# Interleaving the tree block of each token group with the state-space scans of the later groups

## The reference

```
a = in-projection of LN(x); convolution, silu; dt = softplus(...)
for every channel d (256) and state n (16), along the 256 tokens:
    h = exp(dt * A[d,n]) * h + dt * B[n] * u        # the scans
    y[d] += C[n] * h
out1 = LN(x + W_out (y + D*u) * silu(z))

gate = sigmoid(q @ routers.T)                        # the tree, 255 nodes
lp   = product of 8 levels of gate or 1 - gate       # 256 leaves a token
out2 = (lp @ leaf_values) @ Wout + b

4 layers: retention with 8 heads, then gelu(LN(.) @ W1) @ W2
8 experts of one hidden layer, the best by softmax for each token
```

## Time and profile before

| | us |
|---|---|
| median of 3 runs (781.0 to 782.15) | 782.1 |
| the profiled execution, its own time | 781.24 |
| its span, first to last instruction | 779.4 |
| prologue, to the first scan | 76 |
| scans, first start to last end | 190 |
| from there to `rx_stats` of group 3 | 118 |
| from there to the end | 396 |

### The profile page before, as it was taken

How to read it: one execution, slowest core, us unless ns; L and a number is a source line. 1 busy time by engine, 2 the same in 40 slices (tenths; PEclk the granted TensorE clock), 3 DMA queues, 4 the chain that set the end, 5 groups by cost and what they waited for, 6 DMA issues and landing times. The chain is left out here.

```text
span 779.4 us, 13077 instructions
## 1 busy us (share of the span) xinstructions
PE 658.2 (84%) x4791; PEld 430.8 (55%) x4800; DVE 622.9 (80%) x1519; ACT 417.2 (54%) x729; POOL 429.1 (55%) x380
## 2 busy tenths in 40 slices
PE   4997798898988833748899999999999999899994
PEld 1444444444444332634667667777666666667773
DVE  6479798999989686467688888888888888779886
ACT  1996786776767305444454444444444444355551
POOL 6113587696887848464665555555555555551222
PEclk9997799999999986789999999999999999999997
DMA  9003132332344100000000000000000000000001
GB/s 324 7 5 54 35 100 89 86 96 81 84 100 85 55 2 0 0 1 1 2 1 22 1 6 15 22 2 4 15 2 21 2 7 13 1 1 1 1 25 32
DMA packets 17297, 27.36 MB, mean 35 GB/s; under 512 B 2320, under 2 KB 7056, under 8 KB 16976
## 3 DMA queue, kind: packets, MB, share of 16 engines
q1 hardware_dynamic: 17232, 26.51, 12.8%
HBM read 25.32 MB, written 1.18 MB: 34 GB/s over the span
## 5 line engine op out<-in xcount | busy, mean ns | idle before, releaser
L573 POOL TENSOR_TENSOR arena<-arena 128x1024 f32<-128x1024 f32 x64 | 150.0, 2359 | 52.3 <-PE psum L1322 27.3
L991 DVE TENSOR_TENSOR_SCAN arena<-arena,psum 128x1024 f32<-128x1024 f32 x64 | 141.8, 2267 | 3.3 <-issue 2.0
L1322 PE MATMUL psum<-arena,Cs 128*128 128x512 f32 x256 | 121.9, 599 | 1.2 <-POOL arena L573 1.2
L510 POOL TENSOR_TENSOR ve<-mv,eps 128x4 f32<-128x4 f32 x52 | 16.0, 307 | 191.7 <-DVE mv L889 191.7
L705 ACT ACTIVATE arena<-arena 128x510 f32<-128x510 f32 x128 | 84.8, 711 | 51.8 <-DVE arena L991 49.8
L620 POOL TENSOR_TENSOR arena<-arena,mhalf 128x32 f32<-128x32 f32 x16 | 86.8, 5428 | 2.3 <-DVE arena L1108 2.3
L1214 PE MATMUL psum<-Cs,arena 128*128 128x128 f32 x240 | 39.6, 290 | 42.9 <-ACT arena L748 25.9
L1407 PE MATMUL psum<-arena,Wl 128*128 128x512 f32 x128 | 67.4, 639 | 8.6 <-DVE arena L1092 5.3
L1322 PEld LDWEIGHTS psum<-arena,Cs 128*128 128x128 f32 x256 | 45.2, 191 | 46.3 <-issue 35.0
L1214 PEld LDWEIGHTS psum<-Cs,arena 128*128 128x128 f32 x240 | 28.6, 147 | 62.6 <-issue 28.3
L1305 PE MATMUL psum<-Cs,arena 128*128 128x128 f32 x256 | 35.2, 284 | 23.9 <-ACT arena L727 20.7
(11 more groups left out here) (172 smaller groups left out, 1415.6 us busy)
## 6 DMA issues: line engine op xcount, KB each, us to landing
arena<-c_rows_by_state SPq DMA_DIRECT2D x32, 512.0 KB, 4.8
Wl<-wl SPq DMA_DIRECT2D x4, 384.0 KB, 3.2
Wd<-wd SPq DMA_DIRECT2D x1, 1100.0 KB, 10.8
X<-x SPq DMA_DIRECT2D x4, 256.0 KB, 6.4
Sel<-sel SPq DMA_DIRECT2D x1, 1024.0 KB, 8.3
Wl<-wl SPq DMA_DIRECT2D x4, 256.0 KB, 3.0
out<-X SPq DMA_DIRECT2D x4, 256.0 KB, 2.3
Cs<-const SPq DMA_DIRECT2D x1, 614.0 KB, 9.2
```

The costliest lines, as they stand in the source:

```text
L573: pool.tensor_tensor(Hc[:, h], Hs[:, r, h], Crows[:, r], ALU.mult).then_inc(hc_ready, 1)
L991: dve.tensor_tensor_scan(Hs[:, turn % 2, h], Da[:, h], rows_of(turn, h), 0.0, ALU.mult, ALU.add).then_inc(scanned, 1)
L1322: ins = pe.matmul(bank[h], ident, Hc[:, h, group(e)], start=False, stop=False, skip_group_check=True)
```

## The change

**Order.** Scan steps enter `OPENING` as steps of their own, and tree steps are sorted among them: for groups 0 to 2 at 8(g+1) + 1.701 + 0.859 t turns, for group 3 at 33.29 + 0.586 t, where the scans end at 32. The first layer steps start at 31.087 + 3.988 (g + t). All engines follow this list. `TREE_SCHEDULE` has other offsets. `SCHEDULE` has small changes; the cyclic order of `LAYER` on each engine stays as it was.

**PSUM.** Two row buffers, banks 2+3 and 4+5. So the fill of step q+2 waits for scan q. Banks 6 and 7 are the tree's: 7 for `y_proj`, `b_turn`, `b_proj`, both for `logits` and `lp`. At step q PE now adds the states of q-1. `flip` moves from five fills ahead to directly before the last odd turn's fills, and the first one to the front. In the layers `rotate` uses banks 1, 4, 5, 7, and `mix` uses bank 6 alone.

**SBUF.** `Z`, `U`, `Dt`, `Dtu` are stored by group, and a finished group's pieces are used again: `Z` for `Bt` and `LpT`, `U` for `Gates`, `Dt` and `Dtu` for `LpA` and `LpB`; later ones for layer tensors. Shapes of instructions stay. POOL's clearing of `Va` (1.8 us) moves from the tree to before the first layer step.

```diff
+TREE_AT, TREE_PACE = 1.701, 0.859
+LAST_AT, LAST_PACE = 1.290, 0.586
+FIRST_STEPS_AT, FIRST_STEPS_SCALE = 31.087, 3.988
+OPENING = [(what, k, g, 0) for _, _, what, k, g in sorted(
+    [(turn + h / 2, 0, "scan", h, turn) for turn in range(ROUNDS + 1) for h in range(HALVES)]
+    + [(STATE_PAIRS * (g + 1) + TREE_AT + TREE_PACE * t, 1, what, 0, g) for g in range(G - 1) for t, what in TREE_SCHEDULE]
+    + [(STATE_PAIRS * G + LAST_AT + LAST_PACE * t, 1, what, 0, G - 1) for t, what in TREE_SCHEDULE]
+    + [(FIRST_STEPS_AT + FIRST_STEPS_SCALE * (g + t), 2, what, k, g) for g in range(G) for t, what, k in SCHEDULE if g + t < G])]
...
-        row_buffer = [psum[:, (2 + 2 * i) * GC:(4 + 2 * i) * GC] for i in range(3)]
+        row_buffer = [psum[:, (2 + 2 * i) * GC:(4 + 2 * i) * GC] for i in range(2)]
...
-            "rotate": ((1, rotated, 1), (4, rotated, 2), (5, rotated, 3), (1, rotated, 4)),
+            "rotate": ((1, rotated, 1), (4, rotated, 2), (5, rotated, 3), (7, rotated, 4)),
...
+            def scan_step(turn, h):       # PE
+                q = 2 * turn + h
+                if q + 2 < 2 * ROUNDS:
+                    n = FILL_OF[divmod(q + 2, 2)]
+                    if FILL_ORDER[n - 1][0] == "flip":
+                        fill(n - 1)
+                    fill(n)
+                if 1 <= q <= 2 * ROUNDS:
+                    of, half = divmod(q - 1, 2)
+                    if of % STATE_PAIRS == 0:
+                        skip_row(of // STATE_PAIRS, half)
+                    add_states(of, half)
...
                 if what == "b_proj":
                     pe.wait_ge(lp_rows, 2 * g + 2)
-                    if g >= 2:
-                        pe.wait_ge(t2_ready, g - 1)
-                    tokens(bank[6 + g % 2], [LpT[:, g, h, :] for h in range(2)], ...
+                    tokens(hold(7, t2_ready, g + 1), [LpT[g][:, h, :] for h in range(2)], ...
...
-                        pe.wait_ge(*yt_rows.at(layer, g - 2))
+                        rows_y = claim(what, 0, layer, g)
```

More of the change, by code:

```diff
@@ L219 @@
 TURNED = [t for t in range(ROUNDS) if t % 2 == 1]
-FLIP_AHEAD = 6
 def fill_order():
-    fills = []
-    for q in range(2 * ROUNDS):
-        turn, h = divmod(q, 2)
-        g, place = divmod(turn + FLIP_AHEAD // 2, STATE_PAIRS)
-        if h == 0 and place == 0 and 0 < g < G:
+    fills = [("flip", 0, 0)]
+    for turn in range(ROUNDS):
+        g = (turn + 1) // STATE_PAIRS
+        if (turn + 1) % STATE_PAIRS == 0 and g < G:
             fills.append(("flip", g, 0))
-        fills.append(("turned" if turn in TURNED else "rows", turn, h))
-        if q == 1:
-            fills.append(("flip", 0, 0))
+        fills += [("turned" if turn in TURNED else "rows", turn, h) for h in range(HALVES)]
     return fills
@@ L672, in _ @@
                     act.wait_ge(dtx_ready, 2 * g + h + 1)
-                    own.put(act.activation(Hs[:, 1, h, part], Dt[:, h, group(g)], ACT.Abs))
+                    own.put(act.activation(Hs[:, 1, h, part], Dt[g][:, h], ACT.Abs))
                 own.settle()
```

311 lines of the change are left out of this document (153 added, 158 removed).

## The result

| | before | after |
|---|---|---|
| median (us) | 781.97 (781.0 to 782.15, 4 runs) | 801.95 (800.65 to 805.62, 4 runs) |
| span of the profiled execution | 779.4 | 798.9 |
| end of the last scan | 265.7 | 335.5 |
| marker, `rx_stats` of group 3 | 383.2 | 406.9 |
| marker to the end of the span | 396.2 | 392.0 |

The ratio is 1.0255, 95% interval 1.0215 to 1.0295: the change makes the kernel 20 us slower. I had 774.5 and a range that ended at 789. The places were as foretold, their sizes were not. Against my sum the scans end 8.9 later (335.5 for 326.6), the way from there to the marker is 13.4 longer (71.4 for 58), and the layers gain 4.8 less (-4.2 for -9.0). That is 27.1 us, and 774.5 + 27.1 is 801.6.

A forecast was written before the change was run, and what follows sets the result against it. DVE was taken to bound the scans, PE the layers. Scan terms put the scans' end at 326.6; 58 more put the marker 1.4 later; layers -9.0 made -7.6: 773.6 profiled, 774.5 median, range 757 to 789.

The forecast's parts named there:

- Gates, -6.4: Scans: with PE adding one step behind, three gate waits of 2.1 go, -6.4 us (bounds -6.4 and 0).
- Two buffers +4, flips +4.5: Scans: two row buffers lose 0.4 us a pair in ten pairs, +4; three flips delay fills about 1.5 each, +4.5.
- `b_proj`, +8.8: Scans: DVE idles 4.4 us before `b_proj` of groups 0 and 1, waiting for PE, +8.8 (bounds 0 and 8.8).
- Tables, +4.2: Scans, at `logits`: ACT's sigmoid and exponential table loads make decays 2.1 us late, twice, +4.2 (bounds 0 and 7.4).
- Held-up instructions, +13.8: Scans: POOL's products hold up `g_norm` and `levels`, both inputs in SBUF, 2.75 us in each of five blocks, +13.8.
- slower rival: Scans: POOL lags behind queued powers and `low_levels`, two products hold each block, 11.8 more, 786.3 us; chance 0.22.
- Sum of the scans: Scans: 265.7 plus all scan terms, including +32 us of DVE's tree work, puts the last scan's end at 326.6.
- From the last scan to the marker, 58: Behind the scans: group 3's chain alone bounds the way, 58 us; 46 with nothing in the way, 70 with waits doubled.
- Layers, -9.0: Layers: the fourth `rotate` projection's bank wait goes, 0.69 us off each of 13 slots, -9.0 (bounds -9.0 and 0).
- Free gaps: Scans: POOL's products never lie beside `g_norm` and `levels`, so the 13.8 go, 760.7 us; chance 0.20.
- No gain in the layers: Layers: another wait takes the place of the bank's, so -9.0 falls away, 783.5 us, no change; chance 0.10.
- three signs that I had called wrong: Scans' end below 310 or above 340; scans waiting mostly for fills; a layer slot as long as before.

The follow-up runs named there:

- e9: The kernel before with e1's layer banks, and PE adding the states of step q-1 instead of q-2: 770.14 us, ratio 0.9860.
- e1: The kernel before with only the changed kernel's layer bank table (fourth `rotate` projection in bank 7, `mix` in bank 6): 777.00 us, ratio 0.9951.
- e14: The changed kernel with the flips in banks 6 and 7, taking no row buffer: 798.96 us, ratio 1.0226.
- e12: The kernel of e2 with the flips in banks 6 and 7, taking no row buffer: 783.73 us, ratio 1.0028.
- e2: The changed kernel with its whole tree behind the scans, in the order of the kernel before: 794.93 us, ratio 1.0194.
- e6: The changed kernel with the gates of groups 0 and 1 computed by exponential, so no table loads in the scans: 801.27 us, ratio 1.0274.
- e5: The changed kernel with `g_norm` of groups 0 to 2 reading `ln_g` and `ln_b` from PSUM bank 6 instead of SBUF: 794.15 us, ratio 1.0176.
- e10: The changed kernel with all first layer steps sorted behind the marker, `rx_stats` of group 3: 839.82 us, ratio 1.0759.
- e13: The kernel of e10 with matrix products of constants on PE where it stands idle: 832.36 us, ratio 1.0664.
- e3: The changed kernel with DVE's `b_proj` and `t2_stats` of groups 0 and 1 behind the next turn's first scan: 792.09 us, ratio 1.0163.
- e4: The changed kernel with 14 unused bf16 matmuls on PE ahead of each of five fills: 801.76 us, ratio 1.0278.

## Why the prediction was wrong

**What bounds the kernel.** Right. DVE sets the pace of the scans, so all of its tree work is added there: busy time grows by 50.1, of which 32 was foretold and is found. The scan stays at 2.26.

**Gates, -6.4.** Right: the lag of one step takes the 6.4 of waits away and shortens the scans by 7.0 with three buffers (e9 against e1). In the changed kernel the gates' waits fell to 0.8.

**Two buffers +4, flips +4.5.** Close in the changed kernel (9.5 more of waits for fills, flips 4.4 of it by e14), though by luck: without tree work beside them the two are 5.8 and 11.5 (e12, e2).

**`b_proj`, +8.8.** The step that failed is "PE's is behind a bf16 fill and an addition": there were two additions. It measured 11.9. Held to be the upper bound, it was not one.

**Tables, +4.2.** The wait is 4.3, as foretold. Taking it away is worth nothing (e6): other waits and held-up time fill it.

**Held-up instructions, +13.8.** The mechanism is shown (e5), the size was 17.6, and taking 13.2 of it away wins 7.7. Of the slower rival's 11.8 more, 3.8 came. In the rows at 235.60 and 239.87 DVE is held for 5.0: two of POOL's products and an addition of 128x512 (1.31) fall into the block. That happened in two blocks of five. POOL was late there because its product waited 2.21 for PE's addition (the row at 236.03), not because of powers queued among its products.

**Sum of the scans.** From 76.0 on, DVE was idle 11.8 us before (0.3 of the 12.1 lie behind the scans' end), so 26.9 were foretold, and 31.5 are found: +4.6. Busy 223.7 were foretold and 228.0 are found: +4.3, of which 3.8 is held-up time. Together +8.9.

**From the last scan to the marker, 58.** This is the step that failed worst, by 13.4: the chain of group 3 was sized too short. I put it at 46 with nothing in the way, and in the expectation of e10 at 50 with group 2's steps. Without any layer step in the way it took 64.9 (e10), and 60.4 with the granted clock mostly up (e13); in the changed kernel it is 71.4. The term "gates end at 5.8" measured 8.5, which is 2.7 of it. I took every PE step at its length at full clock, though the tree stretch before had a granted clock of 0.82; 1.7 us of that can be seen in the changed kernel. The last power, norm and addition, 5.0, measured 8.1 because layer steps fill DVE up to the marker. What remains is spread over the steps between, and its cause stays open. I named 70 as the bound "with each in-order wait doubled"; the true value was above even that.

**Layers, -9.0.** Half: 0.37 a slot instead of 0.69 (e1). The wait that I read, 0.93, is that of a weight load. PE itself was still at the third projection for a good part of it, so the step that failed is "so 0.69 comes off each slot".

**The rivals.** Free gaps: did not come. Slower: 3.8 of its 11.8. No gain in the layers: half of it came. None had the main cause by itself. But the range left out, in so many words, a slower case in which the chain is long as well, and that is the one that came. None of the three signs that I had called wrong came either: the scans ended between 310 and 340, less than half of DVE's waits were for fills, and a slot was shorter. All three watch the scans and the layers, none the stretch between, where half of the error lay. The terms that missed, `b_proj`, the held-up time, the chain and the layers, all missed towards a longer time. In each a step was taken at its length, or its wait at one hop, and what stood in order ahead of it was counted too short.

## What to carry to other kernels

Work that is moved under a bound engine costs its full length there, and more where an instruction has two SBUF inputs beside a GpSimd product (e5) or stands in order behind another engine (e3). The gain lies in the latency that it leaves behind, so size what remains of that chain first, step by step with the work that each engine still has ahead of it, at the granted clock that the trace shows for such a stretch, and with the other chain that is interleaved with it. Here the chain came out above its upper bound. Look at the parts of a change apart: here the bank table (e1, 0.995) and the shorter lag of the additions (e9, 0.986 with it) are gains that need no interleaving, and the reordering around them lost more than it hid. And the idle time ahead of a weight load is not idle time of PE: read the rows of the matmuls too.

## What the runs showed of the hardware

- Four DVE instructions of 128x128 took 1.10 alone, 4.24 beside POOL's product (and the addition behind it) when all their tensors lie in SBUF, and 1.09 beside the same product when one lies in PSUM (e5).
- After 5.06 us without work TensorE's next fill took 1.97 instead of 1.04 and the addition 3.26 instead of 1.88; with 3.2 us of products of constants ahead both were back at 1.09 and 1.88 (e4). Where PE worked 12 us in 42 the granted clock was 0.50 (e10); with products of constants in the waits, 16.2 of 20 us, it was 0.91 (e13).
- A weight load that waited 0.69 less ended its matmuls only 0.40 earlier (one `rotate` in the kernel before and in e1): the matmul ahead of it, from 506.91 to 507.51, lay beside the wait.
- The same obstacle cost 11.5 us or 4.4, by what else the waiting engine had to do (flips in e2 and e12 against e14).
